# Spline stage of a decoder: gamma and beta by a table product, roots as GpSimd powers

## The reference, cut to what matters

```python
xn = (x - mean) * rsqrt(var + 1e-5) * ln_gamma + ln_beta
slope_sign = sign(mean(spline_slopes, -1))          # of 64 tiles of 4 features
cluster_scores = sign(xn) @ cluster_sigs.T          # 8 clusters of 8 tiles
tile_scores = sign(xn) @ tile_sigs.T
tile_idx = argmax of tile_scores within the best cluster
x_slice = xn[the 4 features of tile_idx]
mn, mx = minimum and maximum of x_slice over all tokens with this tile
u = clip((x_slice - mn) / (mx - mn + 1e-8), 0, 1 - 1e-6)
gi = int(u * 16)
delta = (bases[tile, j, gi] + slopes[tile, j, gi] * (u * 16 - gi)) * output_scale[tile]
return x + (delta at the 4 features of tile_idx, 0 elsewhere)
```

## Time and profile before

| what | us |
|---|---|
| median of 3 runs (lowest, highest) | 3765.04 (3764.64, 3769.51) |
| the profiled execution, and its span | 3769.95, 3768.2 |
| TensorE busy | 3255.4 (86%) |
| VectorE busy | 2812.0 (75%) |
| ScalarE busy | 1987.1 (53%) |
| GpSimd busy | 1132.5 (30%) |

### The profile page before, as it was taken

One profiled execution on the slowest core, in us unless ns is written; L12 is line 12 of the kernel. 1 busy time (PEld: TensorE's weight loads), 2 busy tenths in 40 slices (PEclk: granted clock), 3 DMA queues, 4 the chain that ended last, 5 costly groups with the idle time before them and its releaser, 6 DMA issues. The chain is left out here.

```text
span 3768.2 us, 63508 instructions
## 1 busy us (share of the span) xinstructions
PE 3255.4 (86%) x22659; PEld 2088.0 (55%) x22674; DVE 2812.0 (75%) x5796; ACT 1987.1 (53%) x4818; POOL 1132.5 (30%) x1191
## 2 busy tenths in 40 slices
PE   7899999999862967879899968789999999997775
PEld 3466666666641445645566645555666666664443
DVE  6888988996468675553577858679898898885768
ACT  5577777777631423321444525446666566663555
POOL 2533331264002000000011212106666565653210
PEclk9999999999985988889899979999999999997988
DMA  3433333332110100020000000312222222222000
GB/s 105 101 88 97 91 85 94 88 90 60 39 49 0 37 7 20 2 66 0 23 1 1 1 35 2 128 44 76 82 68 79 73 76 71 78 79 69 2 1 23
DMA packets 245463, 200.88 MB, mean 53 GB/s; under 512 B 114720, under 2 KB 213408, under 8 KB 244256
## 3 DMA queue, kind: packets, MB, share of 16 engines
q1 hardware_dynamic: 245152, 196.82, 17.5%
HBM read 181.39 MB, written 15.34 MB: 52 GB/s over the span
## 5 line engine op out<-in xcount | busy, mean ns | idle before, releaser
L314 PE MATMUL ps<-xT,min 128*128 128x512 f32 (+1 forms) x1072 | 496.1, 608 | 11.8 <-DVE macc L3497 11.4
L3497 DVE SCALAR_TENSOR_TENSOR macc<-ps,mcw,macc 128x508 f32<-128x508 f32 (+2 forms) x408 | 302.6, 742 | 80.1 <-ACT macc L3424 70.3
L3598 POOL TENSOR_TENSOR mSQ<-mSQ,mtn 128x512 f32<-128x512 f32 x128 | 234.7, 1833 | 331.2 <-ACT mtn L3449 331.2
L314 PEld LDWEIGHTS ps<-xT,min 128*128 128x128 f32 (+1 forms) x1072 | 191.0, 189 | 228.2 <-issue 205.7
L3591 POOL TENSOR_TENSOR mE<-mE,mCB 128x1024 f32<-128x1024 f32 x128 | 302.0, 2360 | 44.4 <-DVE mE L3507 26.4
L3507 DVE TENSOR_TENSOR_SCAN mE<-mE,mid 128x1024 f32<-128x1024 f32 x128 | 300.1, 2345 | 0.0
L3357 PE MATMUL ps<-mwo,macc 128*128 128x256 f32 x1024 | 243.0, 380 | 5.4 <-DVE macc L3514 5.4
L3102 DVE TENSOR_REDUCE hMX<-ps 128x2 f32<-128x512 f32 x256 | 165.4, 686 | 109.8 <-PE ps L2989 109.1
L3445 ACT ACTIVATE mtn<-ps,mcol 128x64 f32<-128x64 f32 x1024 | 222.1, 333 | 2.8 <-PE ps L3336 2.8
L3069 ACT ACTIVATE hE<-ps 128x512 f32<-128x512 f32 x256 | 138.9, 595 | 156.4 <-PE ps L2983 156.3
L2983 PE MATMUL ps<-hXE,hKE 32*128 32x256 f32 x1024 | 158.8, 428 | 54.9 <-DVE hMX L3102 40.7
(11 more groups left out here) (591 smaller groups left out, 8177.9 us busy)
## 6 DMA issues: line engine op xcount, KB each, us to landing
mE<-m_decay SPq DMA_DIRECT2D x128, 512.0 KB, 3.6
dE<-d_decay SPq DMA_DIRECT2D x64, 264.0 KB, 3.4
dwk<-in_L_attn_Wk SPq DMA_DIRECT2D x64, 128.0 KB, 2.3
dwq<-in_L_attn_Wq SPq DMA_DIRECT2D x64, 128.0 KB, 2.4
dwv<-in_L_attn_Wv SPq DMA_DIRECT2D x64, 128.0 KB, 2.3
dwg<-in_L_attn_Wg SPq DMA_DIRECT2D x64, 128.0 KB, 2.3
dwo<-in_L_attn_Wo SPq DMA_DIRECT2D x64, 128.0 KB, 2.3
min<-in_m_in SPq DMA_DIRECT2D x2, 4096.0 KB, 18.3
```

The lines of the kernel that those rows point to most:

```text
L314: t = pe.matmul(out, w[:, j, :], self.c.xT[:, j, blk(g, 512)], start=j == 0, stop=j == 1)
L3497: x = dve.scalar_tensor_tensor(out=acc[:, :, 3 - j:T], in0=p[:, :, 0:T - 3 + j], scalar=self.cw[:, i, j:j + 1], in1=acc[:, :, 3 - j:T], op ...
L3598: pool.tensor_tensor(self.SQ[g % 2][:, :], self.SQ[g % 2][:, :], self.tn[s][:, :], ALU.add).then_inc(*self.sqa.up)
```

## The change

- The load gets a fifth transfer: gamma and beta as a table of 64 tiles x 2 x 4 (`gbt`).
- GpSimd's two products per group (XN) are gone; the one-hot product takes XH, the normalised rows, instead.
- A step `affine h` is new: TensorE multiplies the turned one-hot with `gbt`, 8 products with 8 columns, and so finds gamma and beta of the tile of each token. In `range`, VectorE multiplies xs with the one and adds the other (128x32 each), and then signals `slices`.
- `moments` no longer has the root. VectorE signals `var`, and GpSimd computes (var + 1e-5) ** -0.5 by an add and a power: on 128x8 in `stats`, on 128x4 in `close`.
- In `xh`, ScalarE waits for this root between its two passes.
- In `close`, VectorE goes by groups of four: spread, add and moments of the one, then of the other, then the scalings of the one when its root is there, then of the other.

```diff
     def load(self, sp):
-                   (self.tab[:, 0:129], i["s_tab"]), (self.iota[:, :], i["c_iota"]))
+                   (self.tab[:, 0:129], i["s_tab"]), (self.iota[:, :], i["c_iota"]),
+                   (self.gbt[:, :, :], i["s_gb"][0, :, :].rearrange("e (t j) -> t e j", j=4)))
...
         yield "score", 1
+        yield "affine", 0
         yield "oh", 1
+        yield "affine", 1
         yield "range", 0
...
+            elif step == "affine":
+                pe.wait_ge(*room[4 * n])
+                pe.wait_ge(*self.ohc.at(n + 1))
+                for j in range(8):
+                    t = pe.matmul(bank(4 * n)[:, 8 * j:8 * j + 8], self.ohT[n][0:64, j // 4, blk(j % 4)],
+                                  self.gbt[:, :, :].rearrange("t e j -> t (e j)"), start=True, stop=True)
+                t.then_inc(*self.af.up)
+                room[4 * n] = self.xsl.at(n + 1)
...
                 act.wait_ge(own.sem, o)
+                act.wait_ge(*self.root.at(h + 1))
                 for j in range(4 * k, 4 * k + 4):
...
-        def moments(row, st, sw):
-
-            for j in range(8):
+        def moments(row, st):
+
+            n = st.shape[1]
+            for j in range(n):
                 o = own(dve.bn_stats(st[:, j, 0:6], row[:, j, :]))
             dve.wait_ge(own.sem, o)
-            for j in range(8):
-                o = own(dve.bn_aggr(st[:, j, 6:8], st[:, j, 0:6]))
-            dve.wait_ge(own.sem, o)
-            return c.rsqrt(dve, own, st[:, :, 7:8].rearrange("p a b -> p (a b)"), 1e-5, [sw[:, blk(i, 8)] for i in range(3)])
+            for j in range(n):
+                o = dve.bn_aggr(st[:, j, 6:8], st[:, j, 0:6])
+            o.then_inc(*self.var.up)
...
                 dve.wait_ge(own.sem, x)
+                dve.wait_ge(*self.af.at(h + 1))
+                G = bank(4 * h)[:, 0:64].rearrange("p (b e j) -> p b e j", e=2, j=4)
+                then(dve.tensor_tensor(xs, xs, G[:, :, 0, :], ALU.mult))
+                dve.tensor_tensor(xs, xs, G[:, :, 1, :], ALU.add).then_inc(*self.xsl.up)
+                dve.wait_ge(*self.xsl.at(h + 1))
...
             elif step == "close":
-                P2 = self.XH[:, eight, :]
...
+                for g in (2 * h, 2 * h + 1):
+                    four, k = blk(g, 4), blk(g % 2, 4)
+                    P2 = self.XH[:, four, :]
+                    then(dve.tensor_tensor(P2.rearrange("p b (t j) -> p b t j", j=4), self.oh[:, four, :].unsqueeze(3).broadcast_to([128, 4, 64, 4]),
+                                           self.bs[h][:, k, :].unsqueeze(2).broadcast_to([128, 4, 64, 4]), ALU.mult))
+                    then(dve.scalar_tensor_tensor(out=P2, in0=c.X[:, four, :], scalar=2.0, in1=P2, op0=ALU.mult, op1=ALU.add))
+                    moments(P2, self.z8[h][:, k, :])
+                for g in (2 * h, 2 * h + 1):
+                    dve.wait_ge(*self.root.at(g + 3))
+                    for j in range(4 * (g % 2), 4 * (g % 2) + 4):
+                        x = dve.tensor_scalar(c.X[:, 8 * h + j, :], self.XH[:, 8 * h + j, :], self.z8[h][:, j, 6:7], self.zw[h][:, j:j + 1],
+                                              ALU.subtract, ALU.mult)
+                    x.then_inc(*c.xn.up)
...
+        def root(st, w, v, half):
+
+            pool.wait_ge(*self.var.at(v))
+            o = own(pool.tensor_scalar(w[1], st[:, :, 7:8].rearrange("p a b -> p (a b)"), 1e-5, 1.0, ALU.add, ALU.mult))
+            pool.wait_ge(own.sem, o)
+            pool.tensor_tensor(w[0], w[1], half, ALU.pow).then_inc(*self.root.up)
+
         for step, n in self.order():
-            four = blk(n, 4)
-            if step == "w":
-                pool.wait_ge(*self.xh.at(n + 1))
-                o = own(pool.tensor_tensor(self.XN[:, four, :], self.XH[:, four, :], bc(self.gb[:, 0, :], 4), ALU.mult))
-                pool.wait_ge(own.sem, o)
-                pool.tensor_tensor(self.XN[:, four, :], self.XN[:, four, :], bc(self.gb[:, 1, :], 4), ALU.add).then_inc(*self.xb.up)
+            if step == "stats":
+                root(self.s8[n], (self.sw[n][:, 0:8], self.sw[n][:, 8:16]), n + 1, self.half[:, :])
+            elif step == "close":
+                for k in range(2):
+                    root(self.z8[n][:, blk(k, 4), :], (self.zw[n][:, blk(k, 4)], self.zw[n][:, blk(2 + k, 4)]), 3 + 2 * n + k, self.half[:, 0:4])
```

More of the change, by code:

```diff
@@ L1053, in weights @@
         self.gb, self.sl = c.f32("sgb", 2, D), c.f32("ssl", 2, 16)
-        self.tab, self.iota = c.at("stab", [64, 132], F32), c.f32("siota", 96)
+        self.tab, self.gbt, self.iota = c.at("stab", [64, 132], F32), c.at("sgbt", [64, 2, 4], F32), c.f32("siota", 96)
     def load(self, sp):
@@ L1065, in buffers @@
         self.oh, self.xs, self.run = c.f32("soh", NB, 64), c.f32("sxs", NB, 4), c.f32("srun", 2, 2, 64)
-        self.XH, self.W, self.XN, self.PR = (c.f32("s" + n, NB, D) for n in ("XH", "W", "XN", "PR"))
+        self.XH, self.W, self.PR = (c.f32("s" + n, NB, D) for n in ("XH", "W", "PR"))
+        self.half = c.f32("shalf", 8)
         self.pen, self.ts, self.ky, self.cm = (c.sets(2, "s" + n, 8, 64) for n in ("pen", "ts", "ky", "cm"))
@@ L1075, in buffers @@
         t, s, v, p = ((lambda name, n, e=e: self.sig(e, name, n)) for e in ("tensor", "scalar", "vector", "gpsimd"))
-        self.spr, self.tr, self.oht, self.gt = t("signs", 1), t("runs", 1), t("oh", 2), t("gt", 2)
+        self.spr, self.tr, self.oht, self.gt, self.af = t("signs", 1), t("runs", 1), t("oh", 2), t("gt", 2), t("affine", 2)
         self.sgs, self.xh, self.sign, self.ohc = s("sig", 1), s("xh", 4), s("sign", 4), s("oh", 2)
@@ L1079, in buffers @@
             v("sums", 1), v("diag", 1), v("gbs", 1), v("moments", 2), v("xg", 4), v("onehot", 2), v("range", 2), v("tab", 1), v("look", 2))
-        self.xb, self.pr = p("xn", 4), p("pr", 4)
+        self.var, self.xsl = v("var", 6), v("slices", 2)
+        self.root, self.pr = p("root", 6), p("pr", 4)
     def order(self):
@@ L1211, in vector @@
             if step == "slopes":
-                dve.wait_ge(self.dma[0], 64)
+                dve.wait_ge(self.dma[0], 80)
                 dve.tensor_reduce(self.sg[:, :], self.sl[:, :, :], AX.X, ALU.add).then_inc(*self.sums.up)
@@ L1216, in vector @@
                     self.x_rows(dve, g)
-                o = moments(c.X[:, eight, :], self.s8[h], self.sw[h])
-                dve.wait_ge(own.sem, o)
+                moments(c.X[:, eight, :], self.s8[h])
+                dve.wait_ge(*self.var.at(h + 1))
                 dve.tensor_scalar(self.nm[h][:, :].unsqueeze(2), self.s8[h][:, :, 6:7], -1.0, None, ALU.mult).then_inc(*self.mom.up)
@@ L1311, in gpsimd @@
+                for g in (2 * h, 2 * h + 1):
[4 more added lines that the diff above has]
+                    x.then_inc(*c.xn.up)
     def gpsimd(self, pool, own):
         self.before(pool)
-        pool.wait_ge(self.dma[0], 64)
@@ L1314, in gpsimd @@
-        for step, n in self.order():
-            four = blk(n, 4)
-            if step == "w":
-                pool.wait_ge(*self.xh.at(n + 1))
-                o = own(pool.tensor_tensor(self.XN[:, four, :], self.XH[:, four, :], bc(self.gb[:, 0, :], 4), ALU.mult))
-                pool.wait_ge(own.sem, o)
-                pool.tensor_tensor(self.XN[:, four, :], self.XN[:, four, :], bc(self.gb[:, 1, :], 4), ALU.add).then_inc(*self.xb.up)
+        o = own(pool.memset(self.half[:, :], -0.5))
+        pool.wait_ge(own.sem, o)
@@ new lines, in root @@
+        def root(st, w, v, half):
+            pool.wait_ge(*self.var.at(v))
+            o = own(pool.tensor_scalar(w[1], st[:, :, 7:8].rearrange("p a b -> p (a b)"), 1e-5, 1.0, ALU.add, ALU.mult))
+            pool.wait_ge(own.sem, o)
+            pool.tensor_tensor(w[0], w[1], half, ALU.pow).then_inc(*self.root.up)
+        for step, n in self.order():
+            if step == "stats":
[3 more added lines that the diff above has]
+                    root(self.z8[n][:, blk(k, 4), :], (self.zw[n][:, blk(k, 4)], self.zw[n][:, blk(2 + k, 4)]), 3 + 2 * n + k, self.half[:, 0:4])
@@ L1324, in gpsimd @@
                     four = blk(g, 4)
-                    pool.wait_ge(*self.xb.at(g + 1))
+                    pool.wait_ge(*self.xh.at(g + 1))
                     pool.tensor_tensor(self.PR[:, four, :].rearrange("p b (j t) -> p b t j", j=4),
-                                       self.XN[:, four, :].rearrange("p b (t j) -> p b t j", j=4),
+                                       self.XH[:, four, :].rearrange("p b (t j) -> p b t j", j=4),
                                        self.oh[:, four, :].unsqueeze(3).broadcast_to([128, 4, 64, 4]), ALU.mult).then_inc(*self.pr.up)
```

## The result

| what | before | changed |
|---|---|---|
| median of the runs, us | 3765.88 (3764.64 to 3769.51, 4 runs) | 3744.03 (3738.51 to 3750.64, 4 runs) |
| the profiled execution, its span | 3769.95, 3768.2 | 3750.64, 3748.8 |
| VectorE busy | 2812.0 | 2792.8 |
| GpSimd busy | 1132.5 | 1126.3 |

The ratio is 0.9938, with a 95% interval of 0.9926 to 0.9950: 0.6% faster. The forecast was 3746.8. Measured again on the chip of the last experiment the changed kernel had 3748.07 against 3767.34, ratio 0.9945 (0.9933 to 0.9958).

The account below looks back on a forecast made before the run. VectorE's chain of dependent steps was taken to bound the spline stage, with GpSimd's products blocking it. 17.1 - 0.5 + 1.6 = 18.2 us off the 3765.04 median gave 3746.8 us, range 3740.5 to 3754.

Parts of the forecast that it names:

- Part 1: From the spline stage's start to the second one-hot: no Newton chains or blocked VectorE instructions, 17.1 us off.
- Part 2: Table product on TensorE hidden, two new VectorE steps per half in the range: a cost of 0.5 us.
- Part 3: The two closes, by fours with GpSimd roots: 1.6 us off, between bounds of 1.2 and 3.9.
- rival 1: Powers don't block VectorE and the 128x8 power is short: 21.2 us off, 3743.8; chance 0.22.
- The sum: Whole stage: 17.1 - 0.5 + 1.6 = 18.2 us off, giving 3746.8 us.
- Rival 2: GpSimd's root becomes the new bound, 128x8 power slow or pushed back: 13 us off, 3752; chance 0.13.
- Rival 3: TensorE's clock returns much later in the next stage, losing 22.8 us: 3769.6; chance 0.02.
- Rival 4: The stage shortens but the time is hidden: 3764; chance 0.05, shared with a clock giving most back.

Follow-up runs that it names:

- the last experiment: The changed kernel with GpSimd's first one-hot product later and the first close's scalings on ScalarE; 3739.95 us against 3767.34 before, ratio 0.9926.
- table_only: The changed kernel with all roots back on VectorE as Newton steps and the close by eights, table product kept; 3752.80 us against 3767.18 before, ratio 0.9962.
- The probes: The changed kernel plus one scratch GpSimd instruction beside VectorE's work, one execution each: a 128x40 power (3750.15 us) or a 128x2900 multiply (3745.12 us).
- probe_power: The changed kernel plus one GpSimd power on 128x40 scratch data beside VectorE's work on groups 0 and 1; one execution, 3750.15 us.
- late_product: The changed kernel with GpSimd's first one-hot product also waiting for group 3's score input; 3743.45 us against 3767.18 before, ratio 0.9934.

## Why the prediction was right

The number was right because parts 1 and 2, which make up most of it, came out close. In part 3 the forecast took the wrong case: it had GpSimd's powers block VectorE, and they don't. That this left the number within its range is no merit of part 3, since the two cases are only some 3 us apart.

- **Part 1** (17.1 off): 17.70. The mechanism is the one read from the earlier trace rows, and table_only shows it alone. The split that I gave, some 8 us for blocked instructions, 4.8 for the two chains and the rest for ScalarE, was off: with all chains still on VectorE, taking the products away gives 14.07 of the 17.70, because three stalls behind the chain (5.8 us) go too. The powers add 3.6 on top. The power on 128x8 is 1.64 to 1.68 us (I took 1.9 of 1.02 to 2.04) and ScalarE waited 0.37 us for the first root (0.4). The second power lay beside VectorE's group 0 and held nothing up.
- **Part 2** (0.5): 0.45. The table product took 3.55 us per half, near the upper bound of 3.7 although it has 8 columns and not 131. It was hidden: it ended at 1143.14 and 1151.97, and VectorE asked for it at 1147.88 and 1155.18.
- **Part 3** (1.6 off): the step that failed in size. Both closes gave 1.71 + 2.05 = 3.76, the upper of my bounds (3.9). I took a value near the lower, because I put the power in one class with the product that blocks. The probes show that it isn't. This is rival 1, which I gave 0.22.
- **The sum** (18.2): 21.0 in the stage, where rival 1's 21.2 fits best. The medians can't choose: 3744.03 lies at rival 1's 3743.8, and 3748.07 nearer to the forecast of 3746.8. That the profiled executions differ by only 19.3 us is the 1.57 us by which the stage started later.
- **Rival 2** fell with the 1.64 us. **Rival 3**, the clock: the next stage's first 20.4 us have a granted clock of 0.88 as before. The change didn't delay the rise, but when it comes scatters. The eight projections that took 5.78 us before take 5.84 in this trace and 4.21 in the second trace of the same kernel, where the clock of the same stretch is 0.96. The changed kernel's stretch, then those two rows of TensorE:
```profile
1200.50:1220.90 20.40, 19.28 (x56) 10.20 (x55) 9.19 (x14) 6.62 (x14) 3.56 (x2) 0.88 0.51 159
...
1200.85 5.84 PE L314 MATMUL ps<-xT,rw 128*128 128x512 f32 x8
...
1199.16 4.21 PE L314 MATMUL ps<-xT,rw 128*128 128x512 f32 x8
```
- **Rival 4**: the gain was not hidden; instructions of four later stages all moved by 19.3 or 19.4 us.

## What to carry to other kernels

Work on an idle GpSimd is not free while VectorE has work with two SBUF operands or scalings: look for VectorE instructions that end when one of GpSimd's does, before offloading, and put GpSimd's streaming products beside reductions or waits. A chain of tiny instructions is a bad neighbour: each of them can lose a whole product's time. When a step leaves a chain, split the work so that its latency lies beside the other half: by fours VectorE's wait for the root was 0.25 us, by eights 2.05.

## What the runs showed of the hardware

- A GpSimd power costs 1.02 us on 128x4, 1.64 on 128x8 and 6.75 on 128x40, that is about 0.16 us a column and 0.4 fixed. While it runs it doesn't block VectorE's two-operand instructions, nor scalings (probe_power, and the closes); a GpSimd product of about the same length, with 2900 columns, does. The Trainium skill, SBUF — State Buffer, "Who interferes with whom", has every GpSimd instruction that reads SBUF hold the pair for its whole length; for products the trace agrees, for the power of few columns the measurement decides against it (four instructions at 1.23 us under 6.75). Its rule that a reduction doesn't contend agrees with the 2.29 us of late_product.
- GpSimd does wait for VectorE: in the close a 0.20 us add shows 1.08 and a 1.02 us power 1.98.
- GpSimd's memset, which has no input, blocks as well: beside the 2.52 us memsets of probe_product the 128x8 instruction on minus the mean took 1.55 us instead of 0.17 (VectorE's, then GpSimd's timeline):
```profile
1111.29 1.55 DVE L1234 TENSOR_SCALAR snm<-sst 128x8 f32<-128x8 f32 x1
...
1110.29 2.52 POOL L1337 MEMSET sdex<- 128x2900 f32 x1
```
- A TensorE product with 8 columns costs as much as one with 131: 3.55 us for 8 products against 7.3 for 16, 0.44 and 0.46 us each, at a clock of 0.50 in both. TensorE's weight loads are busy for nearly all of either stretch (3.46 of 3.55 us, 7.02 of 7.32).
